# Expert rows of a two-step MoE block rounded up to 128 instead of 256: 110 units in place of 122, with the weight addresses of PE computed in groups

## The reference

```
x = x + 0.5 * ffn(n(x))
x = x + attention(n(x))          # causal, 16 heads of 8 features, then @ WO
x = x + 0.5 * ffn(n(x))          # the same gate and expert weights

ffn(x):                          # 8 experts, hidden size 256, top 2
    probs   = softmax(x @ gate_w.T)
    weights, idx = top_k(probs, 2);  weights /= sum(weights)
    h       = silu(x @ w1[e].T) * (x @ w3[e].T)
    out     = sum over the 2 experts of weight * (h @ w2[e].T)
```

## Time and profile before

| | us |
|---|---|
| median of 3 runs | 637.67 |
| the runs | 635.98 to 640.23 |
| the profiled execution, its own time | 637.84 |
| its span, first to last instruction | 636.1 |
| outside its span | 1.74 |
| mean granted clock of TensorE | 0.956 |

### The profile page before, as it was taken

How to read it: one execution, slowest core, us unless ns; L and a number is a source line. 1 busy time by engine, 2 the same in 40 slices (tenths; PEclk the granted TensorE clock), 3 DMA queues, 4 the chain that set the end, 5 groups by cost and what they waited for, 6 DMA issues and landing times.

```text
span 636.1 us, 20745 instructions
## 1 busy us (share of the span) xinstructions
PE 509.9 (80%) x7774; PEld 395.1 (62%) x7774; DVE 449.6 (71%) x1121; ACT 376.9 (59%) x723; POOL 273.8 (43%) x322
## 2 busy tenths in 40 slices
PE   2769749799798578888789876878787889888894
PEld 2657637678686345555556554645476679777783
DVE  5737955555486877898899898665376646577797
ACT  5847735566465256666666754555564557566674
POOL 7566255750555033434332112454605620565562
PEclk9999988999798779999999999799899989999998
DMA  9981295534965222656313010211144546733232
GB/s 280 320 268 39 81 262 115 136 106 107 180 146 140 79 59 77 171 154 181 87 36 95 36 53 33 89 31 36 36 89 106 129 108 133 155 101 88 66 83 55
DMA packets 124991, 72.27 MB, mean 114 GB/s; under 512 B 51936, under 2 KB 118752, under 8 KB 124896
## 3 DMA queue, kind: packets, MB, share of 16 engines
q1 hardware_dynamic: 117984, 56.78, 33.8%
q0 software_dynamic: 6912, 14.17, 9.0%
HBM read 18.88 MB, written 34.87 MB: 84 GB/s over the span
## 4 chain that ended last, share of the span: by engine, by line
PE 26%; DVE 22%; issue 7%; ACT 4%; DMA 1%; another core or an unknown queue 1%; DVEq 1%; POOL 0%; ACTq 0%; POOLq 0%
DVE negmax L1332 7%; PE bank L1537 4%; PE bank L1535 3%; PE bank L1536 3%; DVE pt L1206 3%; DVE X L1223 2%; PE bank L1666 2%; PE bank L1775 2%; PE bank L1838 2%; PE bank L1658 2%; PE bank L1660 2%; ACT pt L968 1%; DMA yg<-sorted_y,row 1%; PE bank L1853 1%; PE bank L1805 1%
## 5 line engine op out<-in xcount | busy, mean ns | idle before, releaser
L710 POOL DMA_INDIRECT yg<-sorted_y,row x108 | 110.4, 1022 | 147.1 <-PE bank L1814 48.8
L968 ACT ACTIVATE pt<-bank 128x768 f32<-128x768 f32 x128 | 103.8, 811 | 88.1 <-PE bank L1814 85.3
L696 POOL DMA_INDIRECT sorted_x<-xs,row x108 | 115.8, 1072 | 92.7 <-ACT pt L850 27.2
L1214 DVE SCALAR_TENSOR_TENSOR pt<-bank,pt 128x512 f32<-128x512 f32 x122 | 84.2, 690 | 98.4 <-PE bank L1537 43.6
L1332 DVE TENSOR_REDUCE negmax<-bank 128x10 f32<-128x640 f32 x128 | 104.0, 817 | 29.6 <-PE bank L1792 25.9
L844 ACT ACTIVATE pt<-bank 128x512 f32<-128x512 f32 x122 | 73.0, 598 | 40.7 <-PE bank L1537 32.0
L1658 PE MATMUL bank<-w2h,pt 128*128 (+1 forms) x488 | 73.4, 222 | 16.2 <-ACT pt L850 10.6
L1206 DVE TENSOR_TENSOR pt<-pt 128x512 f16<-128x512 f32 x122 | 83.2, 682 | 0.3 <-ACT pt L850 0.3
L850 ACT ACTIVATE pt<-pt 128x512 f16<-128x512 f32 x122 | 76.9, 630 | 4.1 <-DVE pt L1214 3.2
L1660 PE MATMUL bank<-w2l,pt 128*128 (+1 forms) x488 | 72.5, 222 | 2.5 <-issue 2.5
L1775 PE MATMUL bank<-zc 63*64 63x64 f16 (+3 forms) x1024 | 44.1, 250 | 29.5 <-DVE negmax L1332 25.3
(11 more groups left out here) (179 smaller groups left out, 1263.1 us busy)
## 6 DMA issues: line engine op xcount, KB each, us to landing
sorted_y<-yb SPq DMA_DIRECT2D x82, 128.0 KB
zc<-qk_rows SPq DMA_DIRECT2D x96, 64.0 KB
sorted_x<-zeros SPq DMA_DIRECT2D x2, 2944.0 KB
qk_rows<-qksplit SPq DMA_DIRECT2D x8, 512.0 KB
sorted_x<-zeros SPq DMA_DIRECT2D x1, 2432.0 KB, 11.4
sorted_x<-zeros SPq DMA_DIRECT2D x1, 2176.0 KB, 10.1
X<-x_in SPq DMA_DIRECT2D x8, 256.0 KB, 4.9
zc<-w_up SPq DMA_DIRECT2D x8, 256.0 KB, 6.4
```

The lines of the kernel that those rows point to most:

```text
L696: ps.indirect_dma_start(out=sorted_x[s], out_offset=bass.IndirectOffsetOnAxis(ap=row[:, s, k, t:t + 1], axis=0), in_=xs[:, R0[s] + t, :], ...
L710: ps.indirect_dma_start(out=yg[:, a % D_YG, k, :], out_offset=None, in_=sorted_y[s], in_offset=bass.IndirectOffsetOnAxis(ap=row[:, s, k, t ...
L968: s_.activation(pt[:, hg, (u % 2) * 768:(u % 2 + 1) * 768].rearrange("p (a n) -> p a n", a=2), bank[:, B_ST:B_ST + 2, 0:384], ACT.Exp, sca ...
L1214: v_.scalar_tensor_tensor(prod[:, n % D_H], bank[:, B_H3 + n % 2, :], 1.0 / WSCALE, silu[:, n % D_H], ALU.mult, ALU.mult).then_inc(prod_do ...
```

## The change

The rows of each expert are rounded up to 128 instead of 256. A unit still has 256 rows, but its two halves of 128 may belong to two experts. The worst split then needs 31, 39, 39 and 27 halves, so `NT` = (16, 20, 20, 14), 70 routed units instead of 82, and `U_END` is 110. `tile_experts` finds an expert for each half (32 or 40 or 28 halves instead of 19, 23 or 17 units), `places` counts halves. The zero fills of `sorted_x`, its loads and the stores of `sorted_y` shrink with the units. The number of scatters and gathers is the same (108 and 108), and so is the attention.

On PE the up products of a routed unit are made for each half: 24 products with 128 columns instead of 12 with 256. The down products stay 12 with 128 columns. Both halves need their own addresses: 8 for w1, 8 for w3 and 8 for w2. A new function `find` computes those of one weight pair together, ahead of the wait that the products stand behind. Only 4 registers hold offsets; they are loaded for two units at a time, behind the up products of every second unit, 35 loads in all. `first_step`, the pacing of the scatters (6 // 10 for 7 // 10) and gathers, and the places of the attention norm move with the new unit numbers.

```diff
-NT = tuple((2 * n * P + E * (SLOTS - 1)) // SLOTS for n in RT)
+NH = tuple((2 * n * P + E * (P - 1)) // P for n in RT)
+NT = tuple(-(-n // 2) for n in NH)
...
-            return U_TILE[3] + 2 + 9 * d // 13 if p else U_TILE[1] + 2 + 7 * d // 10
+            return U_TILE[3] + 2 + 8 * d // 13 if p else U_TILE[1] + 1 + 6 * d // 10
...
-                    pool.wait_ge(hi_done, done((n - FREE) * 7 // 10, D_H))
+                    pool.wait_ge(hi_done, done((n - FREE) * 6 // 10, D_H))
...
-            def weight_columns(s, count=None):
+            def weight_columns(s):
                 i0 = len(columns[s])
-                i1 = min(NT[s], i0 + (count or NT[s]))
-                if i0 == i1:
-                    return
-                base = Y_TILE[s] - (Y_SECOND if s >= SECOND else 0)
-                regs = [column_regs[(base + i) % COLUMNS] for i in range(i0, i1)]
+                i1 = i0 + PIECE
+                assert i1 <= 2 * NT[s]
                 pe.wait_ge(tiles_done, s + 1)
-                pe.load(regs, woffset[0:1, s, i0:i1])
-                columns[s] += [pe.snap(r, min_val=0, max_val=(E - 1) * HID) for r in regs]
+                pe.load(column_regs, woffset[0:1, s, i0:i1])
+                columns[s] += [pe.snap(r, min_val=0, max_val=(E - 1) * HID) for r in column_regs]
+            def half_of(w, c, column):
+                return w[:, c * P:][:, bass.ds(column, P)]
+            def find(arrays, s, i, held):
+                for u in range(2):
+                    for w in arrays:
+                        for c in range(2):
+                            t_.lower_ap(half_of(w, c, columns[s][2 * i + u]), for_matmul_weights=held)
...
+                    find((wh, wl), s, i, True)
                     pe.wait_ge(read, freed(n))
                     for c in range(2):
-                        cols = bass.ds(columns[s][i] + c * P, P)
-                        last = split_product(bank[:, b0 + n % 2, c * SLOTS:(c + 1) * SLOTS],
-                                             wh[:, cols], wl[:, cols], x[:, 0], x[:, 1])
+                        for u in range(2):
+                            column = columns[s][2 * i + u]
+                            c0 = c * SLOTS + u * P
+                            last = split_product(bank[:, b0 + n % 2, c0:c0 + P],
+                                                 half_of(wh, c, column), half_of(wl, c, column),
+                                                 x[:, 0, u * P:(u + 1) * P], x[:, 1, u * P:(u + 1) * P])
...
+                if i % 2 == 0 and i + 2 < NT[s]:
+                    weight_columns(s)
+                elif i % 2 == 0 and s in (0, 2):
+                    weight_columns(s + 1)
...
+                find((w2h, w2l), s, i, False)
                 pe.wait_ge(y_copied, freed(Y_TILE[s] + i))
-                down(U_TILE[s] + i, columns[s][i])
+                down(U_TILE[s] + i, lambda w, u, c: half_of(w, c, columns[s][2 * i + u]))
```

More of the change, by code:

```diff
@@ L143, in build_macaron @@
         value_row = sb("value_row", [P, 2 * D // 32, 32], F32)
-        bounds = sb("bounds", [P, E, ETILES], F32)
+        bounds = sb("bounds", [P, E, EHALVES], F32)
         before = sb("before", [P, E, E], F32)
-        tile_no = sb("tile_no", [P, NTMAX, E - 1], F32)
+        half_no = sb("half_no", [P, NHMAX, E - 1], F32)
         stats = sb("stats", [P, TILES, 6], F32)
@@ L172, in build_macaron @@
         chosen = sb("chosen", [P, RTMAX + 1, E], BF16)
-        over = sb("over", [P, E, ETILES], F32)
-        ntiles = sb("ntiles", [P, E], F32)
+        over = sb("over", [P, E, EHALVES], F32)
+        nhalves = sb("nhalves", [P, E], F32)
         shares = sb("shares", [P, E, E], F32)
         start = sb("start", [P, E], F32)
-        passed = sb("passed", [P, NTMAX, E - 1], F32)
-        expert = sb("expert", [P, NTMAX], F32)
-        woffset = sb("woffset", [P, SETS, NTMAX + 1], I32)
+        passed = sb("passed", [P, NHMAX, E - 1], F32)
+        expert = sb("expert", [P, NHMAX], F32)
+        woffset = sb("woffset", [P, SETS, NHMAX], I32)
         place = sb("place", [P, RTMAX, E], F32)
@@ L1162, in places @@
                 v_.scalar_tensor_tensor(place[:, 0:n, :],
-                                        start[:, :].unsqueeze(1).broadcast_to([P, n, E]), float(SLOTS),
+                                        start[:, :].unsqueeze(1).broadcast_to([P, n, E]), float(P),
                                         bank[:, B_M0, 0:n * E].rearrange("p (a b) -> p a b", b=E),
@@ L1648, in tile_up, with down @@
                         between()
-            def down(n, offset):
+                if i % 2 == 0 and i + 2 < NT[s]:
+                    weight_columns(s)
+                elif i % 2 == 0 and s in (0, 2):
+                    weight_columns(s + 1)
+            def down(n, weights):
                 q = n % D_HID
@@ L1656, in down @@
                     for c in range(2):
-                        cols = bass.ds(offset + c * D, D)
-                        t_.matmul(dst[u], hidh[:, q, toks[u][c]], w2h[:, cols], start=u + c == 0, stop=False,
+                        t_.matmul(dst[u], hidh[:, q, toks[u][c]], weights(w2h, u, c), start=u + c == 0, stop=False,
                                   skip_group_check=True)
-                        t_.matmul(dst[u], hidh[:, q, toks[u][c]], w2l[:, cols], start=False, stop=False,
+                        t_.matmul(dst[u], hidh[:, q, toks[u][c]], weights(w2l, u, c), start=False, stop=False,
                                   skip_group_check=True)
@@ L1664, in down @@
                     for c in range(2):
-                        cols = bass.ds(offset + c * D, D)
-                        last = t_.matmul(dst[u], hidl[:, q, toks[u][c]], w2h[:, cols], start=False, stop=c == 1,
+                        last = t_.matmul(dst[u], hidl[:, q, toks[u][c]], weights(w2h, u, c), start=False, stop=c == 1,
                                          skip_group_check=True)
@@ L1683, in dense_down @@
                     pe.wait_ge(y_copied, done(sum(NT) - 2 + n, D_Y))
-                down(U_DENSE[p] + n, e * HID)
+                down(U_DENSE[p] + n, lambda w, u, c: w[:, e * HID + c * D:e * HID + (c + 1) * D])
             def experts(s, beside=None):
@@ L1911, in step @@
                                 no_use(pe, use, m1_ready)
-                    if b == ROUTED + 2:
-                        weight_columns(2, PIECE)
-            def second_columns(slot):
-                if slot >= NT[0] - 8:
-                    weight_columns(1, PIECE)
+                    if b == ROUTED + 2 and u == 0:
+                        weight_columns(2)
             def first_groups(n):
```

43 lines of the change are left out of this document (19 added, 24 removed).

## The result

| | before | after |
|---|---|---|
| median, us | 637.34 | 647.38 |
| the runs | 635.98 to 640.23 | 645.6 to 648.66 |
| ratio (95% interval) | | 1.016 (1.012 to 1.020) |
| span of the profiled execution | 636.1 | 646.8 |
| mean granted clock of TensorE | 0.956 | 0.931 |

Slower by 1.6%, where 621 us had been forecast. This is one of two answers: on other Trainium2 chips the same change measured 3% faster. First the trace of the recorded result.

What follows compares the result with a forecast made beforehand. PE was taken to bound a routed unit at 1.98 us, with the excess above that due to indirect DMAs. The terms -23.8 + 1.7 + 3.5 + 1.5 + 1.1 + 0.5 - 1 = -16.5 took 637.8 to 621 us, range 606 to 638.

Steps and rivals of the forecast that it cites:

- the excess: Routed stretches: time above PE's floor, 28.1 and 22.4 us, booked to the indirect DMAs and expected to stay.
- floor: Routed unit's shortest period, with PE alone the limit: 1.98 us before, forecast to become 2.00.
- about 0.6: Routed stretches: us of excess for each indirect DMA of POOL, found alike in the first and second stretch.
- Twelve units, -23.8: Routed parts: six units fewer in each step, each worth 1.98 us, -23.8 us.
- Split products and addresses, +1.7 and +3.5: PE in 70 routed units: 24 short up products cost +1.7 us, 24 register addresses in PE's queue +3.5.
- Set 3 behind its scatters, +1.5 (0 to 5): Set 3's first load waits for its last scatter, its rows now needed by unit 20: +1.5 us.
- four store buffers cover: SP's loads and stores behind set 3's first load shift with it, but six units of loads and four store buffers cover them.
- DVE's end, +1.1: Last dense units: DVE's work rises to 2.36 us a unit, about 1.5 tiles more fall there, +1.1 us.
- A: Routed units: stalls belong to the chain PE, ACT, DVE, PE, so -31.3 replaces -23.8, giving 610 us; chance 0.19.
- B: Routed stretches: POOL and its DMAs set the pace, gathers stay 1.67 us each, half the gain left, 633 us; chance 0.14.
- C: 70 routed units: PE's queue becomes the bound and the kernel slower, 667 us, or 642 in milder form; chance 0.09.
- D: Up products: 128 columns with register address on the stationary side don't keep 0.0555 us, 650 us; chance 0.04.

Runs made afterwards that it cites:

- c2: The kernel before, unchanged, traced on chip 3: 586.38 us (one execution).
- c1: The kernel after, unchanged, beside the kernel before on chip 3: 566.52 against 584.34 us, ratio 0.969.
- e3: Rounding, 82 routed units and pacing of the kernel before, with the new PE program: 585.38 us, ratio 1.005 to the kernel before.
- e2: The kernel after with 12 up products of 256 columns a unit, both halves through the first half's expert: 564.21 us, ratio 0.967 to the kernel before.
- e4: The kernel after with POOL's 104 indirect gathers replaced by plain DMAs of the same size: 561.88 us, ratio 0.963 to the kernel before.
- e1: The kernel after with every weight address of the routed units fixed when the program is written: 565.36 us, ratio 0.972 to the kernel before.
- e12: The kernel after with fixed weight addresses, a second time, on chip 4: 564.65 us, ratio 0.968 to the kernel before.
- e5: The kernel after with set 3's first nine loads three steps later in SP's order, chip 7: 562.45 us, ratio 0.964 to the kernel before.
- e13: The kernel after with set 3's first loads three steps later, a second time, on chip 4: 563.9 us, ratio 0.966 to the kernel before.

## Why the prediction was wrong, and where it was right

**The step that failed** is "I book the excess to the indirect DMAs and what hangs on them, not to the units. Their number stays." In the recorded traces the excess is 50.5 us before, half of it absent on chip 3 with the same scatters and gathers, and 37.2 + 31.7 = 68.9 after. That is +18.4; with the dense units (+9.1), the way to the first routed product (+5.8), attention and tail (-0.9) and the floors' own -21.7 it makes the +10.7 measured. The trace of before had the warning, in PE's timeline of set 0:

```profile
165.64 0.22 PE L1658 MATMUL bank<-w2h,pt 128*128 x1
166.50 0.22 PE L1660 MATMUL bank<-w2l,pt 128*128 x1 [0.64 <-issue]
167.21 0.22 PE L1658 MATMUL bank<-w2h,pt 128*128 x1 [0.49 <-issue]
167.94 0.26 PE L1660 MATMUL bank<-w2l,pt 128*128 x1 [0.52 <-issue]
```

Products of one group, 0.7 to 0.9 us apart, with nothing to wait for: no indirect DMA of POOL ends such a gap. The dividing of 28.1 and 22.4 us by the number of DMAs gave "about 0.6" twice, and that agreement was taken for a cause. What grew in its place is told above: PE's gaps without a wait (15.1 to 29.7 us), the time at the lower clock behind them (15.5 to 44.6 us) and SP's wait ahead of set 3 (2.7 to 10.8 us).

On chip 3 the excess does stay in sum, but not by this account. It is 99.6 - 41 x 1.98 = 18.4 and 86.2 - 40 x 1.98 = 7.0 us before (c2), 25.4 together, and 83.6 - 35 x 2.01 = 13.3 and 80.3 - 34 x 2.01 = 12.0 after (c1), 25.2 together. In the first step it falls by 5.1 us, with as many DMAs, and in the second it rises by 5.0, where SP's new wait is. Two errors cancel there, which is luck. That the first step's part goes with the units, at least in part, shows in e3 on chip 6, where the new program still has 82 of them:

```profile
96.30:196.50 100.20, 92.56 (x1521) 87.00 (x1518) 67.28 (x133) 62.99 (x132) 51.21 (x50) 0.99 0.66 144
```

That is 100.2 - 41 x 2.01 = 17.8 us. Ten traces of 70 units on such chips have 11.8 to 14.5 (floor of 2.01, or 1.98 with whole units), an eleventh, e2, 16.9; all are single executions, so the size is rough. With plain gathers in place of indirect ones (e4) the two stretches take 83.3 and 80.6 us, so that the gathers' look-up is not what the excess pays for.

**Twelve units, -23.8:** measured alone -18.4 and -24.9 on chips 6 and 9, +0.4 on chip 15.

**Split products and addresses, +1.7 and +3.5:** together 2.7 (82 units, chip 6) and 4.1 (chip 9, where half of the addresses is in both). The floor rose by 0.03 us a unit. That is 2.1 us over 70 units; where the rest lies isn't shown. The addresses as such cost nothing to be seen on the chips that e1 and e12 met, so the 3.5 was too much.

**Set 3 behind its scatters, +1.5 (0 to 5):** the right place, undersized, and by another way: ACT waited for a store buffer, not PE for the load. The stores behind SP's wait, which "four store buffers cover", weren't covered: ACT waited 4.16 us for one. The stretch of set 2 and set 3 gave 5.9 us in place of the 10.9 by which the floor fell, and e5 and e13 got 1 to 3.5 us of it back.

**DVE's end, +1.1:** measured +1.9 on chip 3 (50.1 for 48.2). The forecast period was 2.36 us; the one below, with two adds and a dense one, is 2.31, and the mean of the 23 periods 2.18. DVE has no idle time in it:

```profile
528.57 0.69 DVE L1215 SCALAR_TENSOR_TENSOR pt<-bank,pt 128x512 f32<-128x512 f32 x1
529.18 0.68 DVE L1207 TENSOR_TENSOR pt<-pt 128x512 f16<-128x512 f32 x1
529.77 0.42 DVE L1236 TENSOR_TENSOR X<-ot,X 128x256 f32<-128x256 f32 x1
530.11 0.73 DVE L1224 SCALAR_TENSOR_TENSOR X<-yg,weight,X 128x128 f32<-128x128 f32 x2
530.88 0.69 DVE L1215 SCALAR_TENSOR_TENSOR pt<-bank,pt 128x512 f32<-128x512 f32 x1
```

The sum, -16.5, stands beside -17.8, -18.1 and -20.8 on chips 3, 7 and 9, by terms that missed both ways. **Rivals:** A (excess goes with the units) isn't reached as a whole (-27.5 had been its sum), but fits the first step better than the forecast does: six units gone took 0.85 us of excess each, where A had 0.69. B (POOL sets the pace) would have left some 5 us of gain, and 17.8 to 20.8 were measured; its counter-argument had misread, where POOL waits for ACT, a DMA and PE, and not for DVE. C and D are refuted in the steady unit. None of the four, nor the forecast, had the case that came: hold-ups of PE that no wait explains, and that grow with fewer units and with the new program together.

What holds PE up on such a chip isn't settled. Shown: it hits PE's stream and not the other engines' own times; it comes with a third of the semaphore records missing; it is worse for the new PE program, and with fewer units; code loading isn't behind it. Not shown: whether it belongs to the chip at all. No chip was measured a second time, so the chip, its host and the moment can't be told apart. The Trainium skill says of a record queue that is full that by default it drops the new record and, in another mode, stalls the producer (NOTIFIC — Programmer's Manual, When the ring fills); the missing records agree with the first, and whether the recording has any part in PE's gaps, no run here shows. Nor was it tried whether e5, whose edit shortens SP's wait, is faster there.

## What to carry to other kernels

Before an excess is divided by the number of suspects, look at PE's timeline inside it: a gap between two products with no wait belongs to none of them, and a saving in units can vanish into it. Take an excess apart by stage before calling it constant: a sum that stays can be two changes that cancel. Measure a change of 1 to 3% on more than one chip, with the old kernel beside it each time; here the difference itself, and not only the time, changed its sign. And when SP's in-order queue has to wait for something, count who waits for the stores behind it.

## What the runs showed of the hardware that I had not expected

- Two levels of time, by chip: the kernel before takes 582.65 to 585.99 us on chips 3, 4, 6, 7 and 9, and 632.1 to 637.3 on 12, on 15 and in the recorded result, within 1% in each group, at a mean granted clock not far apart (0.970 in c2, 0.956 in the recorded trace). Each chip was measured once.
- In the slower group PE's products come 0.7 us apart, several in a row, with no wait between them.
- Behind such gaps the granted clock falls to 0.50 for 3.4 to 10.2 us at a time, 44.6 us in all in the routed parts and the dense end of the recorded trace of after, and 128-column products then come 0.107 us apart for 0.055.
- The ratio of the two kernels is 0.967 to 0.969 in the one group (chips 3, 7 and 9) and 1.012 to 1.016 in the other (chips 12 and 15 and the recorded result).
- 128-column products with register addresses on the stationary side run at 0.055 us each.
